# Local attention blocks on one core: squares of keys ahead of key copies, result copies ahead of the exponential, probabilities normalised in two pieces

## The reference

```python
def attn_layer(x, Wqkv, qs, ksc, Wo):
    qkv = x @ Wqkv
    q, k, v = jnp.split(qkv, 3, -1)          # 16 heads of 64
    q = l2norm(q) * qs
    k = l2norm(k) * ksc
    q = q * cos * scale + rotate_half(q) * sin * scale
    k = k * cos * inv + rotate_half(k) * sin * inv
    out = local_attention(q, k, v)
    return out @ Wo

def local_attention(q, k, v):
    # windows of 32 queries see their own window and the one before it
    sim = jnp.einsum('bhwie,bhwje->bhwij', bq, bk2) * QK_SCALE
    sim = jnp.where(mask, -jnp.finfo(sim.dtype).max, sim)
    attn = jax.nn.softmax(sim, -1)
    out = jnp.einsum('bhwij,bhwje->bhwie', attn, bv2)
```

## Time and profile before

| | us |
|---|---|
| median of 3 runs (lowest, highest) | 3253.56 (3253.07, 3261.5) |
| the profiled execution's own time | 3262.86 |
| its span | 3260.8 |
| busy in the span: PE | 2822.0 (87%) |
| busy: DVE | 2460.5 (75%) |
| busy: ACT | 2114.0 (65%) |
| busy: POOL | 1310.7 (40%) |

### The profile page before, as it was taken

The page is one execution under the profiler, slowest core; times in us unless marked ns, Lnnn a source line. Parts: engine busy times, 40 slices in busy tenths (PEclk is TensorE's granted clock), DMA queues, the critical chain, the costliest instruction groups (busy, mean ns, idle before and its releaser), DMA issues. The chain is left out here.

```text
span 3260.8 us, 71437 instructions
## 1 busy us (share of the span) xinstructions
PE 2822.0 (87%) x27236; PEld 1709.1 (52%) x27244; DVE 2460.5 (75%) x3103; ACT 2114.0 (65%) x3079; POOL 1310.7 (40%) x923
## 2 busy tenths in 40 slices
PE   5799999996588888888888888888888888779997
PEld 3122222224355555555555555555555555558886
DVE  3899999981388888787887888878888878556664
ACT  2488888883177777777777777777777878511111
POOL 2000000000277566666575657666756666300000
PEclk7799999996699999999999999999999999889998
DMA  3111111100100001000100010001000000000001
GB/s 129 28 29 28 28 28 28 28 19 6 36 30 7 7 14 35 7 7 14 35 7 7 14 35 7 7 14 35 7 7 14 14 7 7 4 27 0 0 0 33
DMA packets 56462, 64.30 MB, mean 20 GB/s; under 512 B 24742, under 2 KB 38964, under 8 KB 55348
## 3 DMA queue, kind: packets, MB, share of 16 engines
q1 hardware_dynamic: 55380, 60.58, 6.9%
q10 hardware_dynamic: 864, 0.79, 0.1%
HBM read 36.69 MB, written 7.34 MB: 14 GB/s over the span
## 5 line engine op out<-in xcount | busy, mean ns | idle before, releaser
L886 DVE TENSOR_REDUCE a_minus_max<-a_ps_max 128x1 f32<-128x1024 f32 x512 | 597.0, 1219 | 58.7 <-PE a_ps_max L811 53.6
L794 ACT ACTIVATE a_expT<-a_ps_scoresT 128x512 f32<-128x512 f32 (+1 forms) x683 | 528.9, 808 | 78.4 <-PE a_ps_scoresT L829 67.7
L1178 POOL TENSOR_TENSOR b_turned_q<-b_rot_q,b_turned_q 128x1024 f32<-128x1024 f32 x96 | 227.6, 2371 | 377.3 <-DVE b_turned_q L1541 377.3
L844 PE MATMUL a_ps_out<-a_expT,v_aug 128*32 128x256 f32 x4096 | 327.9, 392 | 5.4 <-ACT a_outT L781 4.8
L1449 PE MATMUL b_psD<-b_w_qkv,b_xs 128*128 (+1 forms) x384 | 216.2, 651 | 129.4 <-ACT b_outT L1289 129.4
L1276 ACT ACTIVATE b_kT<-b_psD 64x512 f32<-64x512 f32 x384 | 227.4, 592 | 129.7 <-PE b_psD L1366 122.7
L1610 DVE STREAM_TRANSPOSE b_probsT<-b_probs 32x512 f32<-32x512 f32 x384 | 265.6, 692 | 9.0
L765 POOL CAST a_max_hi<-a_minus_max 128x16 bf16<-128x16 f32 x32 | 6.3, 198 | 631.5 <-DVE a_minus_max L886 631.5
L829 PE MATMUL a_ps_scoresT<-a_q_op,a_k_op 26*128 26x512 bf16 x1024 | 247.2, 385 | 13.1 <-ACT a_expT L794 4.4
L1218 POOL TENSOR_TENSOR b_probs<-b_probs,b_inv_sum 128x1024 f32<-128x1024 f32 x96 | 182.8, 1904 | 184.6 <-DVE b_inv_sum L1586 184.6
L1405 PE MATMUL b_psS<-b_kT,b_qT 128*32 128x128 f32 x6144 | 208.5, 277 | 55.6 <-ACT b_kT L1276 55.2
(11 more groups left out here) (296 smaller groups left out, 5896.0 us busy)
## 6 DMA issues: line engine op xcount, KB each, us to landing
b_v_edge<-b_v SPq DMA_DIRECT2D x96, 128.0 KB
b_w_qkv<-L_ffn_Wqkv SPq DMA_DIRECT2D x6, 1536.0 KB
a_q_op<-terms_q SPq DMA_DIRECT2D x128, 48.0 KB
a_k_op<-terms_k SPq DMA_DIRECT2D x128, 48.0 KB
joined<-a_outT SPq DMA_DIRECT2D x256, 16.0 KB
b_w_o<-L_ffn_Wo SPq DMA_DIRECT2D x6, 512.0 KB
a_q_op<-a_max_rows SPq DMA_DIRECT2D x128, 4.0 KB
b_w<-L_ffn_W SPq DMA_DIRECT2D x6, 341.0 KB
```

What stands on the lines that cost most here:

```text
L794: act.activation(expT[:, to:to + 512 * size], ps_scoresT[:, at:at + 512 * size], ACT.Exp, scale=SCALE_A).then_inc(exp_ready, 1)
L844: last_mm = pe.matmul(ps_out[lo:lo + 32, 256 * part:256 * part + 256], v_aug[:, b * T8 + kt, head, :], expT[:, at:at + 256], start=(kt == ...
L886: dve.tensor_reduce(minus_max[p % 2][:, side, 0, qt:qt + 1], ps_max[u % 2][:], AX.X, ALU.max, negate=True).then_inc(max_taken, 1)
L1178: pool.tensor_tensor(turned[:], rot[:], turned[:], ALU.add).then_inc(added, 1)
```

## The change

It moves three things inside the steps and changes no arithmetic. On ACT the square of the keys goes ahead of the four key copies. Both copies to `outT` go ahead of the exponential of the scores, and the first of them also ahead of the one-column exponential. On POOL the normalisation is issued as two instructions, one for each piece of 32 keys, so `probs_ready` now counts 2 for a step; DVE waits for the first piece ahead of L1607 and for the second ahead of L1610. The other waits on `probs_ready` are counted in twos.

```diff
--- before.py
+++ after.py
@@ -1195,7 +1195,7 @@
                     if 1 in lags:
                         pool.wait_ge(unit_k_ready, T)
                     else:
-                        pool.wait_ge(probs_ready, T - 1)
+                        pool.wait_ge(probs_ready, 2 * (T - 1))
                     for j in (2, 3):
                         rows = slice(W * j, W * j + W)
                         pool.tensor_tensor(probsT[W * j - W:W * j, :, rows], packed[rows], ones[rows].unsqueeze(2).to_broadcast([W, HEADS_B, W]),
@@ -1215,8 +1215,9 @@
                 if 1 in lags:
 
                     pool.wait_ge(inv_sum_ready, T)
-                    pool.tensor_tensor(probs[:].rearrange("p h c k -> p h (c k)"), probs[:].rearrange("p h c k -> p h (c k)"),
-                                       inv_sum[:].unsqueeze(2).to_broadcast([P, HEADS_B, 2 * W]), ALU.mult).then_inc(probs_ready, 1)
+                    for c in range(2):
+                        pool.tensor_tensor(probs[:, :, c, :], probs[:, :, c, :],
+                                           inv_sum[:].unsqueeze(2).to_broadcast([P, HEADS_B, W]), ALU.mult).then_inc(probs_ready, 1)
                 if 0 in lags:
                     add(rot_k, turned_k, parts_k_ready, sum_k_ready)
                     unit(rot_k, turned_k, sum_k_ready, unit_k_ready, kT_half, HEADS_B)
@@ -1267,6 +1268,8 @@
                     act.wait_ge(q_ready, T + 1)
                     act.wait_ge(norm2_ready, 2 * T)
                     act.activation(square_q[:], psQ[:], ACT.Square).then_inc(square_q_ready, 1)
+                    act.wait_ge(k_ready, T + 1)
+                    act.activation(square_k[:], psK[:], ACT.Square).then_inc(square_k_ready, 1)
                 if 1 in lags:
 
                     for half in range(2):
@@ -1276,8 +1279,6 @@
                             act.activation(kT[1 - par][rows, 4 * half:4 * half + 4, side, W:W + P],
                                            psD[half][rows, :].rearrange("p (a b) -> p a b", b=P), ACT.Copy).then_inc(kT_held, 1)
                 if 0 in lags:
-                    act.wait_ge(k_ready, T + 1)
-                    act.activation(square_k[:], psK[:], ACT.Square).then_inc(square_k_ready, 1)
                     act.wait_ge(norm2_ready, 2 * T + 2)
                     act.wait_ge(floored_ready, T)
                     act.activation(norm[:], norm2[:], ACT.Sqrt).then_inc(norm_ready, 1)
@@ -1288,17 +1289,17 @@
                     act.wait_ge(out_half, 2 * (T - 2) + half + 1)
                     act.activation(outT[:, 4 * half:4 * half + 4, :].rearrange("p a b -> p (a b)"), psD[half][:], ACT.Copy).then_inc(outT_held, 1)
 
-                if 1 in lags:
-
-                    act.activation(unused[:], res["eps"][:, 0:1], ACT.Exp)
                 if 2 in lags:
                     out_copy(0)
                 if 1 in lags:
 
+                    act.activation(unused[:], res["eps"][:, 0:1], ACT.Exp)
+                if 2 in lags:
+                    out_copy(1)
+                if 1 in lags:
+
                     act.wait_ge(shifted_ready, T)
                     act.activation(probs[:], probs[:], ACT.Exp, scale=QK_SCALE).then_inc(exp_ready, 1)
-                if 2 in lags:
-                    out_copy(1)
                 if ahead:
                     act.wait_ge(w_mlp_in, 16 * 13 * (ahead[0] + 1))
                     norm_start(ahead[0], ahead[1], 0)
@@ -1582,7 +1583,7 @@
                     dve.tensor_reduce(row_sum[:], rows, AX.X, ALU.add).then_inc(sum_ready, 1)
                     dve.wait_ge(sum_ready, T)
                     if 2 in lags:
-                        dve.wait_ge(probs_ready, T - 1)
+                        dve.wait_ge(probs_ready, 2 * (T - 1))
                     dve.reciprocal(inv_sum[:], row_sum[:]).then_inc(inv_sum_ready, 1)
                 if 0 in lags:
                     rotary_sin(psK, turned_k, parts_k_ready, 2)
@@ -1599,12 +1600,13 @@
                     invert(ahead[0], ahead[1], 0)
                 if 1 in lags:
 
-                    dve.wait_ge(probs_ready, T)
+                    dve.wait_ge(probs_ready, 2 * T - 1)
                     if 2 in lags:
                         dve.wait_ge(low_back_ready, 2 * (T - 1))
                         dve.wait_ge(high_back_ready, 2 * (T - 1))
                         dve.wait_ge(out_half, 2 * (T - 1))
                     dve.transpose(packed[:], probs[:, :, 0, :]).then_inc(packed_ready, 1)
+                    dve.wait_ge(probs_ready, 2 * T)
                     for j in range(P // W):
                         rows = slice(W * j, W * j + W)
                         dve.transpose(probsT[rows, :, rows], probs[rows, :, 1, :]).then_inc(probsT_ready, 1)
```

More of the change, by code:

```diff
@@ L1289, in out_copy @@
                     act.activation(outT[:, 4 * half:4 * half + 4, :].rearrange("p a b -> p (a b)"), psD[half][:], ACT.Copy).then_inc(outT_held, 1)
+                if 2 in lags:
+                    out_copy(0)
                 if 1 in lags:
@@ L1294, in step @@
                 if 2 in lags:
-                    out_copy(0)
+                    out_copy(1)
                 if 1 in lags:
```

## The result

The changed kernel takes 3278.61 us (median of 6 runs, 3276.24 to 3294.19), the kernel before, run beside it, 3257.53 us (6 runs, 3245.84 to 3267.17). The ratio is 1.0072 (95% interval 1.0048 to 1.0095): slower by 0.7%, some 21 us. The profiled execution took 3279.3 us for a span of 3277.3. The direction is the one that I forecast; the size is not, since I had put the change at +54 us.

The account below looks back on a forecast made before the run. With no engine full, a ring of waits was taken to set the 17.19 us step. 21 - 1 - 6 - 8 + 48 = +54 us took the profiled 3262.86 to 3317, the median to 3308 us; range 3246 to 3346.

Parts of the forecast that it names:

- The ring behind the result copies: ACT's table load and exponential queue behind `outT` half 0; with POOL's 0.18, +0.29 us a step, +21 us.
- Faster: Rival: the exponential starts early enough that row maximum sets the step, 16.47 us; 60 us less, 3194 us, chance 0.07.
- the branch over the row maximum: Waits from PE's scores to DVE's row maximum: 1.0 to 1.1 us shorter at best with early squares.
- The pieces: POOL's normalisation as two instructions: 2.09 us instead of 1.91, so scaled keys come 0.18 us later each step.
- Edges and turns: Steps beside 11 MLPs: -1 us; at layer turns ACT's unexplained stall mostly hidden, 5 times 1.3: -6 us.
- PE's clock: PE's longer pause ahead of turned keys brings clock falls, +48 us; shorter pauses at the values remove seven, -8 us.
- I take half of the steps at 1.15: +48: PE's 1.8 to 2.0 us pause ahead of turned keys: clock falls in half of 84 steps, 1.15 us each.
- a sign of being wrong: PE's mean grant over the layers staying at 0.99, which would leave 3260 us.
- the lower end of that very term: No clock falls from PE's new pause in 84 steps: 0, in a span of 0 to +92 us.
- The falls that went: PE's pauses at the values shrink to one of about 0.6 us; seven of about 11 falls go: -8 us.
- the first rival: PE's clock holds despite the new pause ahead of turned keys: +6 us remain, 3260 us, chance 0.24.

Follow-up runs that it names:

- squares and pieces: Early squares of the keys and the normalisation in two pieces, against the kernel before, with ACT's old order of result copies: 3194.63 us, ratio 0.9811.
- the two orders: Changed kernel with its table load back ahead of the first copy: 3233.62 us, 0.9895; and with the old copy order, as in squares and pieces: 0.9811.
- two semaphores: Changed kernel with one semaphore for each normalisation piece instead of one that counts twos: 3275.66 us, ratio 1.006 to the kernel before.

## Why the prediction was right in direction and wrong in size

**The ring behind the result copies: right.** I had summed 5.13 us from the end of the key copies to the exponential; the trace has 5.13. DVE waits 1.11 us at the row sum, as put. Against squares and pieces the table load that lost its cover under PE's scores is the main loss (0.65 us a step), the second copy the other (0.46), as the two orders show. "Faster" needed the branch over the row maximum: it exists (16.40 with squares and pieces, where I had 16.47), and the changed kernel isn't on it for the reason named, the place of `outT` half 0.

**The pieces: nearly right, one part missed.** POOL's share came to 0.13 us a step where I had 0.18. The count doubled by the two increments costs DVE 0.09 on the ring, which was not in my sum. Together the step grew by 0.32, not 0.29: 23 us over 72 steps where I had 21.

**Edges and turns: small, and off.** An interval with an MLP and no fall lasts 40.08 to 40.36 us, some 0.3 less than before (40.36 to 40.59, or 40.83 behind a turn): about -3 over 11 where I had -1. At a layer's turn I had won back 1.3 us five times, but only three of the five turns had ever cost anything: four layers run in the loop, and the first and the last stand outside it. At these three ACT's stall is hidden from DVE, as put, but DVE has one of its own in that place. The two steps are 1.1 to 1.5 us longer than two others, much as before (1.2 to 1.5 with a fall's 1.1 taken off), so the -6 became 0. With two semaphores it is there in part: the three turns cost nothing.

**PE's clock: the step that failed.** "I take half of the steps at 1.15: +48." The pause ahead of the turned keys is as long as put, 1.87 us, but no repeated step has a fall: 0, and the mean grant over the layers is 0.99 as before, which the prediction had named as a sign of being wrong. The fault was to set one pause of 1.9 us above two of 0.71 and 0.84 because it is longer than their sum; nothing in the trace had shown a fall behind a pause of this one kind, and the lower end of that very term, none in 84 steps, was what came. Nor did the trace before show that the two pauses make the falls. They stand in each of its steps, and seven steps have a fall: three right behind an interval with an MLP that had a fall itself, three right behind a layer's turn, and one in the first half. The falls that went were worth less net than I had put, too: the seven in steps of before went, but five intervals with an MLP now hold falls (41.6 to 43.2 us, about 11 us in all) where three did (about 5), so clock and all is about -2 instead of -8.

The sum now: 23 - 3 - 2 = +18, against +16.8 between the first and last `b_norm<-b_square_q` of the local blocks (1904.4 us before, 1921.2 after), +16.4 in time of the two profiled executions, and +21 in the medians. Without the +48 the forecast is the first rival, "PE's clock holds", at +6; what parts that from the truth is mostly the turns, the vanished falls and the doubled count. So the direction is in part luck: without the +48 the forecast would have been no change that one can tell from noise, and the sign is right because the gains at the turns and the clock, which were to cancel most of the ring's +21, came to nearly nothing. That the whole is again +21 is chance.

What stays open: whether DVE's stall at a layer's turn is the wait for its code, as the times of the transfers suggest; why the same pause of 2.88 us brings a fall in one step and not in the next, and why copies behind the exponential, with a pause of 1.81 and another of 0.90 in a step, had falls in some steps. The intervals with an MLP show the same: PE's last pauses in them are 0.89 and 1.69 us in each, and three of the eleven have a fall in the kernel before, five in the changed one, eleven with two semaphores. The length of the pauses alone doesn't decide, and I can't say from these runs how several pauses add up.

## What to carry to other kernels

An engine takes its instructions in order: moving a waiting instruction ahead of a table load puts the load on the path, so put loads and other work without inputs ahead of the wait, not behind it. When several edits come together, time them apart: here one was worth 60 us and another took it all and more. A semaphore for each piece, waited for by the plain step count, was cheaper on this ring than one with a doubled count: 0.09 us in a step, and a stall less at three turns.

The version to keep is early squares, two pieces with a semaphore each, and the copies where they were: 3177.65 us, a ratio of 0.975, or 76 us by the medians.

## What the hardware showed that I had not expected

- A wait on a computed count (`2 * (T - 1)`) between two dependent instructions of DVE costs 0.09 us more than one on `T - 1` (1.34 against 1.25 us). The trace shows the register instruction between them, with the wait for the first of the two on it (1787.82, the reciprocal at 1787.90).
- The grant of PE's clock answered steeply to the length of one pause: no fall behind 1.87 us, one in two behind 2.88, nearly each behind 3.88. Yet two pauses of 0.71 and 0.84 us, less than 1.87 together, stood ahead of some falls in the kernel before and with the pieces alone, and passed without one in most steps.
- A table load costs its 1.28 us and no more even where it stands on the ring: in the changed kernel the next instruction starts 1.30 us after the load does (1783.60 to 1784.90), and the load 0.01 us after the copy ahead of it ends. The Trainium skill (ScalarE: Activation LUTs, What ACT_TABLE_LOAD costs) puts a switch at about 2.66 us with a drain; no kernel here shows that drain, and the measurement decides.
